# A quantised MLP layer: the state kept in fp32, its residual put in the bank by transposes, and each engine given its own order

## What is computed

```
h = x
for blk in range(3):
    y = linear(h, q[2*blk], ...)          # weights: 4-bit, scaled in groups of 16, plus a rank-32 product
    y = gelu(layernorm(y) * gamma + beta)
    h = linear(y, q[2*blk+1], ...) + h
out = layernorm(x + h)                    # the wrapper
```

## Time and profile before

| | |
|---|---|
| time before, median of 3 runs | 2795.01 us (2794.78 to 2800.27) |
| the profiled execution's own time | 2797.56 us |
| its span | 2795.7 us |
| the quantised layer in it | from 864 us to about 2248 us; its steps from 957 us |
| granted TensorE clock, mean | 0.971 |

### The profile page before, as it was taken

How to read it: one execution, slowest core, us unless ns; L and a number is a source line. 1 busy time by engine, 2 the same in 40 slices (tenths; PEclk the granted TensorE clock), 3 DMA queues, 4 the chain that set the end, 5 groups by cost and what they waited for, 6 DMA issues and landing times. The chain is left out here.

```text
span 2795.7 us, 39684 instructions
## 1 busy us (share of the span) xinstructions
PE 2620.3 (94%) x13416; PEld 2085.5 (75%) x13416; DVE 1748.8 (63%) x2920; ACT 1234.0 (44%) x2351; POOL 695.9 (25%) x1029
## 2 busy tenths in 40 slices
PE   6999999999995999999999999999999959999998
PEld 4777777777772578778787877878787747777776
DVE  2456465464564666666666666666666647777777
ACT  3334334343341344334334344343433447777775
POOL 2123122122230011111120111112111115556555
PEclk9999999999996699999999999999999979999999
DMA  3111112112115100001010100101010042222231
GB/s 109 46 61 51 69 60 75 45 60 79 41 45 126 43 0 31 31 1 62 1 62 1 42 20 1 61 1 62 1 62 1 10 153 87 95 90 90 90 113 68
DMA packets 91981, 149.91 MB, mean 54 GB/s; under 512 B 18300, under 2 KB 21124, under 8 KB 91716
## 3 DMA queue, kind: packets, MB, share of 16 engines
q1 hardware_dynamic: 79184, 144.78, 15.1%
q10 hardware_dynamic: 12660, 3.32, 0.7%
HBM read 97.76 MB, written 50.33 MB: 53 GB/s over the span
## 5 line engine op out<-in xcount | busy, mean ns | idle before, releaser
L1187 PE MATMUL quant_bank<-quant_W_hi,quant_h_hi 128*128 128x512 f32 x768 | 312.7, 407 | 11.5 <-ACT quant_bank L1076 11.2
L1037 POOL TENSOR_SCALAR quant_var<-quant_mv 128x1 f32<-128x1 f32 x256 | 56.2, 219 | 1072.1 <-DVE quant_mv L1103 1072.1
L1188 PE MATMUL quant_bank<-quant_W_lo,quant_h_hi 128*128 128x512 f32 x768 | 303.4, 395 | 0.0
L1189 PE MATMUL quant_bank<-quant_W_hi,quant_h_lo 128*128 128x512 f32 x768 | 303.2, 395 | 0.0
L1071 ACT ACTIVATE quant_h_hi<-quant_h_sum 128x512 fp32r<-128x512 f32 x128 | 81.0, 632 | 472.3 <-DVE quant_h_sum L1140 472.3
L1507 DVE TENSOR_TENSOR mlp_g_lo<-mlp_g,mlp_g_hi 128x512 fp32r<-128x512 f32 x256 | 231.6, 918 | 85.9 <-ACT mlp_g_hi L1447 85.1
L1101 DVE BATCH_NORM_STATS2 quant_stats<-quant_bank 128x6 f32<-128x512 f32 x192 | 133.8, 697 | 153.9 <-PE quant_bank L1189 152.8
L1123 DVE TENSOR_TENSOR quant_g_lo<-quant_bank,quant_g_hi 128x512 fp32r<-128x512 f32 x192 | 132.7, 691 | 135.6 <-ACT quant_bank L1065 135.4
L1444 ACT ACTIVATE mlp_g<-mlp_p_h,mlp_b 128x512 f32<-128x512 f32 x256 | 177.1, 692 | 91.6 <-PE mlp_p_h L1547 62.5
L1215 PE MATMUL quant_bank<-quant_g_hi,quant_W_hi 128*128 128x512 f32 x512 | 205.2, 401 | 0.0
L1217 PE MATMUL quant_bank<-quant_g_lo,quant_W_hi 128*128 128x512 f32 x512 | 202.5, 396 | 0.0
(11 more groups left out here) (229 smaller groups left out, 6447.6 us busy)
## 6 DMA issues: line engine op xcount, KB each, us to landing
delta_x_in<-L_attn_x_d SPq DMA_DIRECT2D x16, 1024.0 KB, 6.2
delta_x_res<-L_attn_x_d SPq DMA_DIRECT2D x16, 1024.0 KB, 7.5
x_d<-delta_z SPq DMA_DIRECT2D x16, 1024.0 KB, 5.1
quant_x_in<-x_d SPq DMA_DIRECT2D x16, 1024.0 KB, 5.7
x_d<-quant_y SPq DMA_DIRECT2D x16, 1024.0 KB, 5.5
mlp_x_in<-x_d SPq DMA_DIRECT2D x16, 1024.0 KB, 9.8
mlp_x_res<-x_d SPq DMA_DIRECT2D x16, 1024.0 KB, 8.1
out_d<-mlp_z SPq DMA_DIRECT2D x15, 1024.0 KB, 5.1
```

Source lines behind the costliest of these rows:

```text
L1187: mm(out, x_hi, W_hi[:, 2 * b, k, :], start=False, stop=False, skip_group_check=True)
L1188: mm(out, x_hi, W_lo[:, 2 * b, k, :], start=False, stop=False, skip_group_check=True)
L1189: last = mm(out, x_lo, W_hi[:, 2 * b, k, :], start=False, stop=k == KT - 1, skip_group_check=True)
```

## The change

- **State.** The transposed state `h` is kept in fp32 in the buffer of `x_in`, which `enter` has read by then. `h_sum` goes. In block 0 VectorE still makes the new state from `h_hi` and `h_lo` in two additions, in block 1 in one, from `h`.
- **Residual.** In `leave`, four fp32 transposes of `h` with `start` on the first put the state into the bank, in place of ScalarE's seed and the 8 fp32r products. The last bias is added to `h` by ScalarE beforehand, in `up` of block 2. `ident_r` and one row of `b_all` go.
- **The row x of the last addition** is loaded a second time, into `y`, once `turn` of block 2 has read it; the next `x_in` is loaded once TensorE has finished `leave`.
- **Orders.** TensorE does the first quarter of a `down` or `leave` piece, the `head`, before the `turn` that stood in front of it (five turns of a step). ScalarE does its part of `down(.,.,1)` after the first chunk of the following `turn`, not before it. VectorE does its part of `down(.,.,2)` between chunks 1 and 2 of the `turn`, not after chunk 3.
- **Preparation.** TensorE's loop over layers is written out.

The core of the diff:

```diff
+        ORDER_PE, ORDER_DVE = list(ORDER), list(ORDER)
+        TURNS = [(1, b, 0, b) for b in range(LAST)] + [(0, b + 1, 1, b) for b in range(LAST)]
+        for m, b, m_down, b_down in TURNS:
+            ORDER_PE.insert(ORDER_PE.index(("turn", m, b, 0, 0)), ("head", m_down, b_down, 2, 0))
+            ORDER_DVE = moved(ORDER_DVE, ("down", m_down, b_down, 2, 0), ("turn", m, b, 1, 0))
+        ORDER_PE.insert(ORDER_PE.index(("turn", 1, LAST, 0, 0)), ("head", 0, LAST, 2, 0))
...
+        for m, b, m_down, b_down in TURNS:
+            ORDER_ACT = moved(ORDER_ACT, ("down", m_down, b_down, 1, 0), ("turn", m, b, 0, 0))
+
+        def h(m, k):
+
+            return x_in[m][:, k, :]
...
             def load(t, m):
-                sp.wait_ge(S[m]["z_done"], RT * t)
+                sp.wait_ge(S[m]["z_ps"], RT * t)
                 sp.dma_start(x_in[m][:, :, :], rows(x1, t, m)).then_inc(x_in_dma[m], 16)
+
+            def load_residual(t, m):
+                sp.wait_ge(S[m]["yT_ps"], KT * BLOCKS * (t + 1))
+                sp.dma_start(y[m][:, :, :], rows(x1, t, m)).then_inc(y_in_dma[m], 16)
...
             with sp.Fori(0, STEPS - 1) as t:
                 for m in range(STREAMS):
+                    load_residual(t, m)
+                for m in range(STREAMS):
                     load(t + 1, m)
                     store(t, m)
...
+            def up(t, m, b, k):
+
+                if b == LAST:
+                    s = S[m]
+                    act.wait_ge(s["h_lo_done"], KT * (BLOCKS * t + b) + k + 1)
+                    nc.scalar.activation(h(m, k), h(m, k), ACT.Identity, bias=b_col[:, 2 * b + 1, k:k + 1]).then_inc(s["h_biased"], 1)
...
                 dve.wait_ge(s["mlp_ps"], n)
-                nc.vector.scalar_tensor_tensor(h_sum[:, k % 2, :], lin_of["down", m, b, k][:, :], b_col[:, 2 * b + 1, k:k + 1], as_f32(h_hi[m][:, k, :]),
-                                               ALU.add, ALU.add).then_inc(s["h_part"], 1)
-                dve.wait_ge(s["h_part"], n)
-                nc.vector.tensor_tensor(h_sum[:, k % 2, :], h_sum[:, k % 2, :], as_f32(h_lo[m][:, k, :]), ALU.add).then_inc(s["h_new"], 1)
+                old = h(m, k) if b else as_f32(h_hi[m][:, k, :])
+                nc.vector.scalar_tensor_tensor(h(m, k), lin_of["down", m, b, k][:, :], b_col[:, 2 * b + 1, k:k + 1], old, ALU.add, ALU.add).then_inc(s["h_part"], 1)
+                if b == 0:
+                    dve.wait_ge(s["h_part"], n)
+                    nc.vector.tensor_tensor(h(m, k), h(m, k), as_f32(h_lo[m][:, k, :]), ALU.add).then_inc(s["h_new"], 1)
...
+                if r == 0:
+                    dve.wait_ge(y_in_dma[m], 16 * t + 16)
                 dve.wait_ge(s["z_ps"], RT * t + r + 1)
-                nc.vector.tensor_tensor(y[m][:, r, :], lin_of["leave", m, b, r][:, :], x_in[m][:, r, :], ALU.add).then_inc(s["z_done"], 1)
+                nc.vector.tensor_tensor(y[m][:, r, :], lin_of["leave", m, b, r][:, :], y[m][:, r, :], ALU.add).then_inc(s["z_done"], 1)
...
-                for k in range(KT):
-                    mm(out[:, k * P:(k + 1) * P], h_hi[m][:, k, span], ident_r[:, :], start=False, stop=False, skip_group_check=True)
-                    mm(out[:, k * P:(k + 1) * P], h_lo[m][:, k, span], ident_r[:, :], start=False, stop=False, skip_group_check=True)
...
+            def leave_residual(t, m, b, r):
+
+                lin_free(pe, t, "leave", m, b, r)
+                if r == 0:
+                    pe.wait_ge(S[m]["h_biased"], KT * t + KT)
+                out = lin_of["leave", m, b, r][:, :]
+                for k in range(KT):
+                    mm(out[:, k * P:(k + 1) * P], h(m, k)[:, r * P:(r + 1) * P], ident[:, :], start=k == 0, stop=False, is_transpose=True, skip_group_check=True)
...
+            def head(t, m, b, i):
+
+                if b == LAST:
+                    leave_residual(t, m, b, i)
+                    leave_part(t, m, b, i, range(1))
+                else:
+                    lin_free(pe, t, "down", m, b, i)
+                    down_part(t, m, b, i, range(1))
```

More of the change, by code:

```diff
@@ L753, in quantised_mlp_layer @@
         x_in_dma = [sem(f"x_in_dma_{m}") for m in range(STREAMS)]
+        y_in_dma = [sem(f"y_in_dma_{m}") for m in range(STREAMS)]
         def rows(dram, t, m):
@@ L896, in layer @@
                         lora(l + 1, k)
-                layer(0)
-                with pe.Fori(1, LAYERS - 1) as l:
+                for l in range(LAYERS - 1):
                     layer(l)
@@ L1047, in leave @@
                 scale_of(t, m, BLOCKS, r, 1.0 + LN_EPS, LN_EPS * LN_EPS)
[L1049 removed]
+            run(pool, {"up": up, "leave": leave}, ORDER)
         @block.scalar
@@ L1158, in leave @@
                                             ALU.subtract, ALU.mult).then_inc(s["x3_done"], 1)
-            run(dve, {"enter": enter, "up": up, "turn": turn, "down": down, "leave": leave})
+            run(dve, {"enter": enter, "up": up, "turn": turn, "down": down, "leave": leave}, ORDER_DVE)
         @block.tensor
@@ L1217, in down, with leave_part @@
                     last = mm(out, W_hi[:, 2 * b + 1, k, cols], g_lo[m][:, k, :], start=False, stop=k == KT - 1)
[L1218 to L1220 removed]
+                return last
+            def down(t, m, b, j):
+                headed = ("head", m, b, j, 0) in ORDER_PE
+                if not headed:
+                    lin_free(pe, t, "down", m, b, j)
+                down_part(t, m, b, j, range(headed, KT)).then_inc(S[m]["mlp_ps"], 1)
+            def leave_part(t, m, b, r, chunks):
                 s = S[m]
                 out = lin_of["leave", m, b, r][:, :]
[L1224 removed]
                 span = slice(r * P, (r + 1) * P)
[L1226 to L1229 removed]
+                for k in chunks:
                     if r == 0:
@@ L1234, in leave @@
                     last = mm(out, g_lo[m][:, k, span], W_hi[:, 2 * b + 1, k, :], start=False, stop=k == KT - 1, skip_group_check=True)
-                last.then_inc(s["z_ps"], 1)
-            run(pe, {"enter": enter, "up": up, "turn": turn, "down": down, "leave": leave})
+                return last
+            def leave_residual(t, m, b, r):
[5 more added lines that the diff above has]
+                    mm(out[:, k * P:(k + 1) * P], h(m, k)[:, r * P:(r + 1) * P], ident[:, :], start=k == 0, stop=False, is_transpose=True, skip_group_check=True)
+            def leave(t, m, b, r):
+                headed = ("head", m, b, r, 0) in ORDER_PE
+                if not headed:
+                    leave_residual(t, m, b, r)
+                leave_part(t, m, b, r, range(headed, KT)).then_inc(S[m]["z_ps"], 1)
+            def head(t, m, b, i):
+                if b == LAST:
+                    leave_residual(t, m, b, i)
+                    leave_part(t, m, b, i, range(1))
+                else:
+                    lin_free(pe, t, "down", m, b, i)
+                    down_part(t, m, b, i, range(1))
+            run(pe, {"enter": enter, "up": up, "turn": turn, "down": down, "head": head, "leave": leave}, ORDER_PE)
 def low_rank_mlp_layer(nc, x3, w, consts, out):
```

68 lines of the change are left out of this document (28 added, 40 removed).

## The result

The changed kernel takes 2723.73 us (median of 4 runs, 2720.73 to 2727.76); the kernel before, on the same chip, 2797.64 us (4 runs, 2794.78 to 2802.59). The ratio is 0.9735, 95% interval 0.9713 to 0.9757. The gain, 73.9 us, is 15 us more than the 59 forecast; 2.6 of these come from the median of before, which stood at 2795.01 us when the forecast was made.

A forecast was written before the change was run, and what follows sets the result against it. TensorE's own stream plus its waits was taken to bound a step. Residual 3.1 and waits 4.3 make 7.4 us a step, times 8 = 59 us: 2797.6 to 2738.6, by the median 2736; range 2725 to 2768.

The forecast's parts named there:

- the residual: In `leave`, four fp32 transposes replace eight small products: gain 0.38 us a row, 3.1 us a step with switches.
- the waits: TensorE's waits before `turn`, `up` and `leave(0,2,0)`, and on `h_lo`, all go: 4.3 us a step.
- 1.05 + 1.94 + 0.50: Losses a step before three `turn` pieces, before `up` for its seeds, and before `leave(0,2,0)` for its seed, in us.
- The eight stretched products before `h_lo`: In `up`, records of 0.49 instead of 0.40 us show waits on `h_lo` parts: eight a step, 0.84 us.
- 4 x 0.104 + 0.08 = 0.50: Price in us of a `leave` row's four transposes: 0.104 each from sixteen plain ones, 0.08 for the next product's delay.
- share the switch: Two `leave` rows right after transposes save +0.16 us; the head before the last `turn` adds a switch, -0.08.
- two single improvements: For the low end: the first turn's wait also goes (0.35 us), new transposes cost no switch (0.64): 8.4 a step.
- The hand schedule and the covers: Queues followed at `turn(1,0)`: nothing late, slack 0.6 us in three places; `h` biases and extra loads cost nothing.
- B: Rival, chance 0.12: TensorE stops at late `g_lo` or `h_lo` instead; only the residual is gained, 25 us: 2770.
- C: Rival, chance 0.07: loads of y1, `x_in[0]` and y0's store slow each other, `enter` waits: 2748, at worst 2788.
- D: Rival, chance 0.04: transposes in an open group take four passes, a row's residual 1.84 us: 27 us slower, 2822.
- E: Rival, chance 0.02: 20 transposes together lower the clock; 5 us a step at half clock gives 2776.

The follow-up runs named there:

- e5: Changed kernel with the residual by eight fp32r products again, last bias left out: 2749.69 us, period 155.85 us.
- e12: Changed kernel with TensorE's preparation kept as a loop over the layers: 2719.89 us, period 152.17 us.
- e2: Changed kernel with ScalarE in its old order, the other two engines in the new ones: 2714.37 us, period 152.19 us.
- e1: Changed kernel without TensorE's five heads, its order as before: 2724.53 us, period 153.34 us.
- e3: Changed kernel with VectorE in its old order, `down(.,.,2)` after all four chunks of `turn`: 2727.61 us, period 153.57 us.
- e10: Kernel before with only the three new orders and the heads, old seeds, small products and additions kept: 2767.97 us, mean period 157.13 us.

## Why the prediction was right, and where it was short

The direction and the mechanisms came out as forecast, and the time lies below the stated range, because two terms of the sum were too small: the residual (3.1 where 3.67 was measured) and the waits (4.3 where 5.05 was measured).

**TensorE's own stream and its waits are what a step is made of: right.** The steps carry 68.2 of the 69.8 us between the spans.

**The waits of 4.3 us a step: right in kind, too small.** From 155.85 (e5, in which only the residual is as before) to 160.90 it is 5.05. The large ones were sized well: summed from start to start, the intervals before the bracketed waits lose 3.78 us before and 0.34 after, 3.44; forecast were 1.05 + 1.94 + 0.50 = 3.49. What is left of the 5.05 is 1.6, where 0.84 stood. The eight stretched products before `h_lo` were sized well too: they are nine, and 0.92 us. About 0.7 us was put at nothing. It lies in stalls of 0.05 to 0.1 that no bracket shows. Two places of before show them, at an `up` and at a row of `leave`:

```profile
1486.20 0.40 PE L1189 MATMUL quant_bank<-quant_W_hi,quant_h_lo 128*128 128x512 f32 x1
1486.51 0.50 PE L1187 MATMUL quant_bank<-quant_W_hi,quant_h_hi 128*128 128x512 f32 x1
...
1424.98 0.40 PE L1234 MATMUL quant_bank<-quant_W_hi,quant_g_lo 128*128 128x512 f32 x1
1425.32 0.32 PE L1227 MATMUL quant_bank<-quant_ident_r,quant_h_hi 128*128 128x128 f32 x1
1425.48 0.28 PE L1228 MATMUL quant_bank<-quant_ident_r,quant_h_lo 128*128 128x128 f32 x1
```

The products at 1486.51 and 1425.32 start 0.31 and 0.34 us after their forerunners, at a pace of 0.233, and the first small product takes 0.16 to its successor, where an undelayed one takes 0.06. Compared with e5, a step of before loses 0.15 us in three intervals like the first, 0.1 in the one before 1425.32, 0.17 in the first transposes of the three late `turn`s (0.165 instead of 0.109) and 0.3 in first small products. Nothing in a table of waits shows those; only the sum of all intervals over a period does.

**The residual of 3.1: the mis-sized price.** It measured 3.67 (e5), 0.46 a row instead of 0.38. The step that failed is "4 x 0.104 + 0.08 = 0.50". Four cost 0.35 + 0.08 = 0.43 us: three intervals of 0.109, one of 0.03 to the next product, and the switch. The 1.67 us of 16 transposes hold that short last interval once in 16; the prediction's mean spread it over all of them, and so gave a group of four only a quarter of what it saves (0.02 of 0.08 us). With the switch added, a group of n costs about n x 0.109, which also leaves nothing for rows that "share the switch" (+0.16 and -0.08 in the prediction). The earlier trace rows held this: the group's record is 1.91 long and a single transpose's 0.27, so 15 intervals take 1.64 us, 0.109 each. The small products of before, put at 0.88 us, are 8 x 0.112 = 0.90.

**The sum.** 0.57 + 0.75 = 1.3 us a step, 8 x 1.32 = 10.6 us, where the forecast for the profiled execution, 2738.6, and its 2727.8 are 10.8 apart. That the two agree to 0.2 is partly luck: the eight steps together gained 68.2 us, 9 more than forecast, and the rest came from outside them. By medians the distance is 12.3; the 1.5 us more are within what the last layer adds by chance.

**The range.** Its low end, 2725, was built from the same mean price and the same count of small waits, with two single improvements on top, and it left out that the rest of the program moves by several microseconds from run to run. Either end would have needed that width.

**The hand schedule and the covers: right.** The eight times above; no wait beside that of `turn(0,0)` appeared, so ScalarE's biases and the two loads are covered, and the unrolled loop gave nothing that shows (e12). The prediction left open which of the three orders does the work: VectorE's and the heads do (1.39 and 1.16), ScalarE's doesn't beside these two (e2).

**The rivals.** B, the waits only move: none did. C, the loads: the landings are 5.5 and 5.6 us, though the DMA share rose from 0.07 to 0.12, and `enter` never waits for them. D, four passes: four transposes into an open bank take 0.35 us, not 1.76. The Trainium skill, "FP8 and Floating Point Precision", TensorE Precision Notes, gives true fp32 four passes; transposes don't pay them here: 0.109 us each, where an fp32 product of that size takes 1.18 / 4 = 0.30. E, the clock: 1.00 over the whole step with 20 transposes in a row. The Trainium skill, "TensorE: Matmul & The Clock Gate", Part 4, doesn't count transposes as work for the clock gate; groups of up to 2.1 us between products left the granted clock at 1.00 here.

**What stays open.** Why GpSimd's additions and VectorE's subtractions meet badly in 3 of 16 steps in one execution and in 12 in another wasn't tried, nor why the clock falls behind some of the waits and not behind others. That shorter additions remove both the stretching and most of the spread is shown; that the two engines contend for memory is only argued from the timeline. The stalls of 0.7 us a step are counted, but which of the orders or the dropped instructions removes each of them wasn't separated.

## What to carry to other kernels

Price a small group of instructions by its intervals, one by one, and look at the first and the last of them: n instructions have n - 1 equal intervals and an odd one, and a mean over a long run hides the odd one. Where one engine is the bound, add up all start-to-start intervals over one period and compare with the bare pace: here the stalls of 0.05 to 0.1 us that no bracket shows weigh 0.7 us a step, as much as two of the waits before `turn`. And measure such a change by its period: e1 and e3 cost 9 and 11 us and didn't show in the medians, since a layer that nobody touched moved by more. Take the mean of several periods: in e10 a single one was off by 0.5 us.

## What the runs showed that was not expected

In a group of fp32 transposes between fp32r products each 128x128 block starts 0.109 us after the one before, the product behind starts 0.03 us after the last, and that product's successor comes 0.08 late: about 0.109 us for each block in all, for groups of 4, 8 and 16. Products can be accumulated onto a bank that such transposes opened, at no further cost.

GpSimd's additions of 128x512 fp32 (about 1.3 us each) stretched VectorE's subtractions of the same size from 0.69 to as much as 4.6 us: a subtraction that started 1 us into the first of four additions in a row ended only behind the fourth, while the additions kept their pace. It happened in a varying part of the last layer's steps. With the short additions the layer took 24 to 31 us less than in these two profiles (534.1 against 503.4 in the changed kernel, 527.7 against 503.4 in its repeat); part of that is the granted clock, which fell to 1.2 GHz for 3.4 us behind some of the waits of 1.8 us.
